# Attention begun with batch 0 alone; the other batches' residual, norm and turn, and the second feed-forward's norms, in pieces inside the slots

## The chip, the cores and the metric

One Trainium2 chip, one core. The metric is the device time of one execution in microseconds (us); the time before is the median of three runs. "Slot", "batch" and "half" are words of this kernel and are explained below.

## What is computed

A macaron block on x of 8 batches x 512 tokens x 128 features, all in fp32 accuracy:

```
x = x + 0.5 * ffn(layernorm(x))        # first feed-forward
x = x + attn(layernorm(x), Q, K, VO)   # 16 heads, softmax over 512 keys
x = x + 0.5 * ffn(layernorm(x))        # second feed-forward, same weights
ffn: 3 blocks of  h = h + lin2(gelu(layernorm(lin1(h))))
lin: dequantised 4-bit weight + low-rank part (folded into one 128 x 128 weight)
```

## The kernel before, in words

Every engine has its own program, written out by hand, and they meet on counting semaphores; there is no scheduler. x stays in SBUF as 32 tiles of 128 tokens, four tiles to a batch.

**Feed-forward.** `ffn(f)` is a software pipeline of 12 steps (3 blocks x 4 pairs of batches), one pair of batches a step. A step has `lin1`, `turn_z` and `lin2` on TensorE (PE), `squares` and `gelu` on ScalarE (ACT), `seed`, `z_scaled` and `step_h` on VectorE (DVE), and three Newton steps for 1/sqrt on GpSimd (POOL, `newton`: small linked operations on `u_t`, `u_u`, `u_rstd`). Ahead of it each batch is normalised (`norm_stats`, `norm_means`, `norm_sigmas`, `norm_apply`) and turned by four PE transposes (`pre`); behind it it is turned back (`post`) and added to x (`step_x`). Batches go in two groups of four.

**Between the first feed-forward and attention** batches 0 to 3 get `step_x`, their norm, `turn_xn` and their split in fp16 high and low halves (`halves_turned`, `split`, `halves_tokens`, `xn_low`); only then does attention start. Batches 4 to 7 are normalised in its first slots, and turned in slots 0 to 3.

**Attention** runs in slots, one head of one batch each, 128 in all, with six more ahead (-6 to -1) that fill the pipeline. PE's slot k has, in this order: `scores` of head k+1 (8 matmuls), `outputs` of head k-1 (12 small ones), `weigh` of head k (12, in pieces `weigh(0)` to `weigh(3)`), `maxima` for head k+4 or so (4) and one `project` (3): 39 matmuls. DVE's slot k has `row_max` of head k+2 (four stream transposes into `head_ops`), `scale_out`, two `reduce_max` (they follow `maxima` of the same slot), `y_low` of head k, and the low half of a projection. ACT's slot k has `exps` and `p_high` of head k+1, a projection's high half and `y_high` of head k. POOL's slot k has `add_out` of head k-3 (x plus the head's output) and `p_low` of head k, in two halves; `plo_done` counts them, and PE waits for the first ahead of `weigh(0)` of slot k. Since `exps` and `p_high` of head k are done in ACT's slot k-1, POOL's slot k lies about two thirds of a slot ahead of PE's slot k. Slots 4 to 119 are a hardware loop over four slots.

**Behind attention** the same DVE statements compute the norms of all 8 batches for `ffn(1)`: batches 0 to 3 in the last slots, 4 to 7 behind `lin1` of the first two steps.

Of the kernel before, what the change touches and what calls it, by code (L numbers as in the profile page):

```python
# [21 lines left out]
def macaron(nc, x_d, q_d, k_d, vo_d, qw_d, sc_d, bias_d, la_d, lb_d, gam_d, bet_d, out_d):  # L22
# [10 lines left out]
    GT = SG * TT  # L33
# [13 lines left out]
    with ctx:  # L47
# [42 lines left out]
        stats = sb("stats", [128, GT, 6])  # L90
        mv = sb("mv", [128, 2, GT, 2])
        var = sb("var", [128, GT])
        rs_t = sb("rs_t", [128, GT])
        rs_u = sb("rs_u", [128, GT])
        rstd = sb("rstd", [128, 2, GT])
        shift = sb("shift", [128, 2, GT])
# [35 lines left out]
        bank = [ps[:, b, :] for b in range(B)]  # L132
# [3 lines left out]
        pj_ps = ps[:, 5, :]  # L136
        o_ps = ps[:, 6:8, 0:2 * RW].rearrange("p b (t n) -> p b t n", n=RW)
# [24 lines left out]
        xhat_a = sem("xhat_a")  # L162
        pre_t = sem("pre_t")
# [42 lines left out]
        late_ps = ps[:, 6, :]  # L206
        top_rows = ps[0:NTOP, 0, 0:128]
        top_cols = ps[:, 2, 0:NTOP]

        def wait_xhat(eng, u, c):  # L210

            if c < SG // 2:
                eng.wait_ge(xhat_v, u * (SG // 2) + c + 1)
            else:
                eng.wait_ge(xhat_a, (u - 1) * (SG // 2) + c + 1)
# [25 lines left out]
        def _(sp):  # L241
# [60 lines left out]
            for b in range(B):  # L302
                sp.wait_ge(x1_ready, B + b + 1)
                sp.dma_start(ov[:, b * TT:(b + 1) * TT, :], x[:, b * TT:(b + 1) * TT, :]).then_inc(out_sem, 16)
# [4 lines left out]
        def _(pool):  # L309
# [39 lines left out]

            pool.wait_ge(prep_p, 8)  # L350
# [7 lines left out]
            pool.wait_ge(prep_a, 3)  # L358
            pool.tensor_tensor(w_lo[:, :, :], qk32[:, :, :], w_hi[:, :, :], ALU.subtract).then_inc(prep_p, 1)
            pool.wait_ge(prep_a, 5)  # L360
            pool.tensor_tensor(vo_lo[:, :, :], vo32[:, :, :], vo_hi[:, :, 0:D], ALU.subtract).then_inc(prep_p, 1)

            def xn_low(b):
                tiles = slice(b * TT, (b + 1) * TT)
                pool.wait_ge(xnh_ready, b + 1)
                pool.tensor_tensor(xn_lo[:, tiles, 0:D - 1], xhat[:, tiles, 0:D - 1], xn_hi[:, tiles, 0:D - 1],
                                   ALU.subtract).then_inc(xnl_ready, 1)

            for b in range(SG):
                xn_low(b)  # L370

            def p_low(k, par, a):
                pool.wait_ge(phi_done, 2 * k + (a + 1))
                rows = slice(2 * a, 2 * a + 2)
                pool.tensor_tensor(p_lo[:, par, rows, :], p32[:, par, rows, :], p_hi[:, par, rows, :],  # L376
                                   ALU.subtract).then_inc(plo_done, 1)

            def add_out(k, par, batch):
                pool.wait_ge(o_scaled, k + 1)  # L380
                rows = x[:, bass.ds(batch * TT, TT), :]
                pool.tensor_tensor(rows, rows, o_sb[:, par, :, :], ALU.add).then_inc(x_added, 1)  # L382

            def slot(k, j, add_batch):
                if not isinstance(k, int) or k >= 3:
                    if not isinstance(k, int) or k >= 4:
                        pool.wait_ge(x_added, k - 3)
                    add_out(k - 3, (j + 1) % 2, add_batch)
                for a in range(2):
                    if not isinstance(k, int) or k >= 2:  # L390
                        pool.wait_ge(av_half, 2 * (k - 2) + (a + 1))
                    p_low(k, j % 2, a)

            slot(0, 0, 0)
            slot(1, 1, 0)
            xn_low(SG)
            slot(2, 0, 0)
            xn_low(SG + 1)
            slot(3, 1, 0)  # L400
            xn_low(SG + 2)
            xn_low(SG + 3)
            with pool.Fori(1, NH // 4) as i:
                for j in range(4):
                    slot(4 * i + j, j, (4 * i + (j - 3)) // H)
            for k in range(NH - 3, NH):
                pool.wait_ge(x_added, k)
                add_out(k, k % 2, k // H)
            for i in range(STEPS):
                newton(1, i)  # L410

        @block.scalar
        def _(act):
# [7 lines left out]
            def pre(f, s):  # L421
                for c in range(SG):
                    b = s * SG + c
                    act.wait_ge(pre_t, f * B + b + 1)
                    nc.scalar.activation(hT[:, b, :], bank[b], ACT.Copy).then_inc(h0_ready, 1)

            def norm_apply(u, s, batches=range(SG // 2, SG)):

                act.wait_ge(moments_ready, u + 1)
                for c in batches:  # L430
                    for t in range(c * TT, (c + 1) * TT):
                        ins = nc.scalar.activation(xhat[:, s * GT + t, :], x[:, s * GT + t, :], ACT.Identity,
                                                   scale=rstd[:, s, t:t + 1], bias=shift[:, s, t:t + 1])
                    ins.then_inc(xhat_a, 1)

            def squares(f, i):
                for c, b in unit_batches(i):
                    act.wait_ge(lin1_done, at(f, i, c))
                    for t in range(TT):
                        cols = slice(t * D, (t + 1) * D)  # L440
                        ins = nc.scalar.activation(work_b[:, b, cols], bank[b][:, cols], ACT.Square,
# [3 lines left out]
            def gelu(f, i):  # L445
                n = i // UNITS
                for c, b in unit_batches(i):
                    act.wait_ge(z_turned, at(f, i, c))
                    nc.scalar.activation(work_a[:, b, :], bank[b], ACT.Gelu, scale=gam[:, n:n + 1],
                                         bias=bet[:, n:n + 1]).then_inc(gl_ready, 1)  # L450

            def weight_halves(i):

                if i == 7:
                    act.wait_ge(prep_v, 3)
                if i in (7, 8):
                    n = i - 7
                    ins = nc.scalar.activation(w_hi[:, n, :], qk32[:, n, :], ACT.Identity, scale=inv2[:, n:n + 1])
                if i == 9:
                    ins = nc.scalar.activation(vo_hi[:, :, 0:D], vo32[:, :, :], ACT.Identity, scale=inv2[:, 2:3])  # L460
                    ins.then_inc(prep_a, 1)
                if i == 10:
                    act.wait_ge(prep_a, 2)
                    for n in range(2):
                        ins = nc.scalar.activation(qk32[:, n, :], qk32[:, n, :], ACT.Identity, scale=inv2[:, n:n + 1])
                    ins.then_inc(prep_a, 1)
                if i == 11:
# [3 lines left out]
                    nc.scalar.activation(vo32[:, :, :], vo32[:, :, :], ACT.Identity,  # L471
                                         scale=inv2[:, 2:3]).then_inc(prep_a, 1)

            def halves_tokens(u, b):
                wait_xhat(act, u, b % SG)
                tiles = slice(b * TT, (b + 1) * TT)
                nc.scalar.activation(xn_hi[:, tiles, 0:D - 1], xhat[:, tiles, 0:D - 1], ACT.Copy).then_inc(xnh_ready, 1)

            def halves_turned(b, src):
                act.wait_ge(xn_t, b + 1)  # L480
                nc.scalar.activation(xt_hi[:, b, :], src, ACT.Copy).then_inc(xth_ready, 1)

            def ffn(f):
                if f == 0:
                    norm_apply(0, 0)
# [6 lines left out]
                for i in range(STEPS + 3):  # L492
                    if i >= 3:
                        gelu(f, i - 3)
# [663 lines left out]
```

## Time and profile before

| | |
|---|---|
| median of 3 runs | 1027.19 us (1026.61 to 1031.52) |
| the profiled execution: its own time / its span | 1026.52 us / 1024.7 us |
| PE busy | 963.4 us, 94% |
| DVE busy | 877.1 us, 86% |
| ACT busy | 802.6 us, 78% |
| POOL busy | 784.4 us, 77% |
| PE's share of the chain that ended last | 83% (DVE 10%, ACT 3%, POOL 2%) |
| granted TensorE clock, mean | 0.979 |

The span is the profiled program from its first to its last instruction; the execution's own time is 1.8 us longer. [...] Times in rows are counted from the span's start.

### The profile page before, as it was taken

The page shows a single profiled execution, that of the slowest core. Times are in us where ns is not written, and L with a number is a line of the kernel's source. Part 1 is how long each engine was busy: PE and PEld are TensorE (multiplying, and loading weights), DVE is VectorE, ACT ScalarE, POOL GpSimd, SP SyncE. Part 2 cuts the span into 40 slices and gives each one's busy share as a digit, 9 for nine tenths or more (in the row PEclk, how much of TensorE's full clock was granted, in tenths as well). Part 3 has the DMA queues.
Part 4 walks back from the last instruction along what each step waited for, and adds up shares of the span by engine and source line. Part 5 has one row for each costly group of instructions (what it writes and reads, how often), then busy time and mean ns, then how long its engine had stood idle before and what let it go on. Part 6 is the DMA issues. An engine that isn't in the chain of part 4 may idle for free.

```text
span 1024.7 us, 22051 instructions
## 1 busy us (share of the span) xinstructions
PE 963.4 (94%) x5892; PEld 502.3 (49%) x5892; DVE 877.1 (86%) x1786; ACT 802.6 (78%) x1293; POOL 784.4 (77%) x706
## 2 busy tenths in 40 slices
PE   4895689999999999999999999999999999997897
PEld 4763234444444444444444444444444444444775
DVE  7667898988888889898888888888888888898566
ACT  4885388888888888888888888888888888886874
POOL 2644168888888888888888888888888888886442
PEclk9999699999999999999999999999999999998999
DMA  9000222222222222222222222222222222220002
GB/s 244 1 2 0 51 50 55 62 61 62 63 63 64 64 65 63 64 64 63 63 64 65 63 64 61 61 61 61 61 61 61 61 61 61 61 62 1 1 1 83
DMA packets 71676, 59.03 MB, mean 58 GB/s; under 512 B 11168, under 2 KB 70560, under 8 KB 71648
## 3 DMA queue, kind: packets, MB, share of 16 engines
q1 hardware_dynamic: 71392, 58.31, 24.0%
q10 hardware_dynamic: 256, 0.39, 0.1%
q8 instruction: 12, 0.20, 0.1%
q14 instruction: 16, 0.13, 0.0%
HBM read 6.23 MB, written 2.10 MB: 8 GB/s over the span
## 4 chain that ended last, share of the span: by engine, by line
PE 83%; DVE 10%; ACT 3%; POOL 2%; issue 1%; DMA 1%; SPq 0%; DVEq 0%; POOLq 0%; ACTq 0%
PE ps L1032 11%; PE ps L1034 10%; PE ps L1033 10%; PE ps L1022 10%; PE ps L1023 10%; PE ps L1015 6%; PE ps L1007 3%; PE ps L953 3%; PE ps L1048 3%; PE ps L1044 3%; PE ps L1045 3%; PE ps L1009 3%; PE ps L1008 3%; PE ps L925 2%; DVE stats L654 1%
## 5 line engine op out<-in xcount | busy, mean ns | idle before, releaser
L376 POOL TENSOR_TENSOR p_lo<-work_b,p_hi 128x1024 f16<-128x1024 f32 x256 | 539.8, 2130 | 129.4 <-ACT p_hi L527 129.3
L794 DVE TENSOR_REDUCE mcol<-ps 128x2 f16<-128x1024 f32 x256 | 301.0, 1220 | 0.8 <-PE ps L1015 0.7
L522 ACT ACTIVATE work_b<-ps,exp_scale 128x1024 f32<-128x1024 f32 x256 | 271.6, 1111 | 32.4 <-PE ps L1023 32.3
L527 ACT ACTIVATE p_hi<-work_b 128x1024 f16<-128x1024 f32 x256 | 256.0, 1054 | 0.0
L1022 PE MATMUL ps<-head_ops 128*128 128x512 f16 x512 | 195.1, 381 | 4.1 <-DVE mcol L794 2.0
L1032 PE MATMUL ps<-p_hi,xn_hi 128*128 128x512 f16 x512 | 195.2, 381 | 0.0
L1023 PE MATMUL ps<-head_ops 128*128 128x512 f16 x512 | 195.1, 381 | 0.0
L1033 PE MATMUL ps<-p_hi,xn_lo 128*128 128x512 f16 x512 | 194.4, 380 | 0.0
L1034 PE MATMUL ps<-p_lo,xn_hi 128*128 128x512 f16 x512 | 194.3, 379 | 0.0
L382 POOL TENSOR_TENSOR x<-x,o_sb 128x512 f32 (+1 forms) x128 | 162.7, 1271 | 8.7 <-DVE o_sb L819 8.7
L804 DVE STREAM_TRANSPOSE head_ops<-mcol 32x128 f16<-32x128 f16 x512 | 155.5, 304 | 9.3
L532 ACT ACTIVATE y_hi<-ps 128x512 f16<-128x512 f32 x128 | 76.5, 598 | 90.0 <-PE ps L1034 89.8
L810 DVE TENSOR_TENSOR y_lo<-ps,y_hi 128x512 f16<-128x512 f32 x128 | 88.5, 691 | 60.5 <-ACT y_hi L532 60.4
L1044 PE MATMUL ps<-vo_hi,y_hi 128*128 (+1 forms) x512 | 93.8, 221 | 5.6 <-DVE o_sb L819 5.6
L819 DVE TENSOR_TENSOR o_sb<-ps,rinv 128x512 f32<-128x512 f32 x128 | 88.4, 691 | 7.0
L1048 PE MATMUL ps<-vo_hi,y_lo 128*128 (+1 forms) x512 | 93.9, 221 | 0.3 <-DVE y_lo L810 0.2
L1045 PE MATMUL ps<-vo_lo,y_hi 128*128 (+1 forms) x512 | 93.8, 220 | 0.0
L1015 PE MATMUL ps<-pair_ops 64*128 64x512 f16 x512 | 79.8, 386 | 8.0 <-DVE mcol L794 4.9
L1022 PEld LDWEIGHTS ps<-head_ops 128*128 128x128 f16 x512 | 50.2, 98 | 68.8 <-issue 6.5
L1034 PEld LDWEIGHTS ps<-p_lo,xn_hi 128*128 (+1 forms) x512 | 50.2, 98 | 60.8 <-issue 0.6
L1023 PEld LDWEIGHTS ps<-head_ops 128*128 128x128 f16 x512 | 50.2, 98 | 59.6 <-issue 0.8
L1032 PEld LDWEIGHTS ps<-p_hi,xn_hi 128*128 (+1 forms) x512 | 50.1, 98 | 59.5 <-issue 22.1
(116 smaller groups left out, 1316.9 us busy)
## 6 DMA issues: line engine op xcount, KB each, us to landing
head_ops<-pair_ops SPq DMA_DIRECT2D x512, 64.0 KB, 2.0
head_ops<-pair_ops SPq DMA_DIRECT2D x128, 128.0 KB, 2.4
x<-x_dram SPq DMA_DIRECT2D x8, 256.0 KB, 5.9
out<-x SPq DMA_DIRECT2D x8, 256.0 KB, 3.0
vo_last<-wvo_dram SPq DMA_DIRECT2D x1, 1024.0 KB, 13.5
qk<-wq_dram SPq DMA_DIRECT2D x1, 512.0 KB, 5.6
qk<-wk_dram SPq DMA_DIRECT2D x1, 512.0 KB, 6.4
scl<-scales_dram ACTq DMA_DIRECT2D x8, 48.0 KB, 5.2
```

Of the source, the lines that this page charges most:

```text
L376: pool.tensor_tensor(p_lo[:, par, rows, :], p32[:, par, rows, :], p_hi[:, par, rows, :], ALU.subtract).then_inc(plo_done, 1)
L382: pool.tensor_tensor(rows, rows, o_sb[:, par, :, :], ALU.add).then_inc(x_added, 1)
L522: nc.scalar.activation(p32[:, par, 2 * a:2 * a + 2, :], s_ps[a], ACT.Exp, scale=exp_scale[:, 0:1]).then_inc(exp_done, 1)
L527: nc.scalar.activation(p_hi[:, par, 2 * a:2 * a + 2, :], p32[:, par, 2 * a:2 * a + 2, :], ACT.Copy).then_inc(phi_done, 1)
L794: nc.vector.tensor_reduce(mcol[:, par, :, t, 0], s_ps[t % 2], AX.X, ALU.max, negate=True).then_inc(max_red, 1)
L804: ins = nc.vector.transpose(rows[:, :, 32 * q:32 * q + 32], mcol[32 * q:32 * q + 32, par, e, :, :])
L1015: ins = nc.tensor.matmul(s_ps[t % 2][:, e, :], pair_ops[half, buf, 0, t * 128:(t + 1) * 128], pair_ops[half, buf, 2, :], start=True, stop= ...
L1022: nc.tensor.matmul(s_ps[a][:, u % 2, :], k1[:, ring, keys], q1[:, ring, :], start=True, stop=False)
L1023: ins = nc.tensor.matmul(s_ps[a][:, u % 2, :], k2[:, ring, keys], q2[:, ring, :], start=False, stop=True)
L1032: nc.tensor.matmul(y_ps, xh, p_hi[:, par, u, :], start=(u == 0), stop=False)
L1033: nc.tensor.matmul(y_ps, xl, p_hi[:, par, u, :], start=False, stop=False)
L1034: ins = nc.tensor.matmul(y_ps, xh, p_lo[:, par, u, :], start=False, stop=(u == TT - 1))
```

## The change

The functions `attn_slot(n)` and `ffn_slot(m)` give for every batch the slot at which its pieces begin, and each engine's new `late(k)` does the pieces that fall on slot k, at one place inside its slot. Batch 0 alone is finished between the first feed-forward and attention. The last two steps of the first feed-forward overlap slots -6 to -4. The first two `lin1` steps of the second feed-forward run inside slot 127. All slots are written out (no loop), on all engines but the DMA queue. In the slots the norm's 1/sqrt is split: DVE does the variance and the first guess (`late_seed`), POOL three Newton steps in five parts, one part a slot (`late_newton`), ACT applies it. The last group's norm and the eight `step_x` of the second feed-forward are reordered. ACT's scaling of the attention weights goes to DVE.

```diff
+        def attn_slot(n):
+            return 16 * (n - 1) - 8 if n > 1 else -3
+        def ffn_slot(m):
+            return 16 * (m + 1) + 5
+        SEEDS = sorted([(attn_slot(n) + 4, "attn", n) for n in range(1, B)] +
+                       [(ffn_slot(m) + 2, "ffn", m) for m in range(B - 1)])
...
 # POOL
+            def late_newton(kind, b, part):
+                tiles = slice(b * TT, (b + 1) * TT)
+                y, v = rstd[:, tiles], var[:, tiles]
+                if part == 0:
+                    if seeded(kind, b) > 1:
+                        pool.wait_ge(nrstd_ready, seeded(kind, b) - 1)
+                    pool.wait_ge(nseed_ready, seeded(kind, b))
+                for n in range(3 * part, min(3 * part + 3, 12)):
+                    if n % 4 == 0:
+                        plink(pool, pool.tensor_tensor(n_t[:, :], y, y, ALU.mult))
...
+            def late(k):
+                for part in range(5):
+                    for n in late_at(k, 4 + part, "attn"):
+                        late_newton("attn", n, part)
+                    for m in late_at(k, 2 + part, "ffn"):
+                        late_newton("ffn", m, part)
+                for h in range(2):
+                    for n in late_at(k, 11 + h, "attn"):
+                        xn_low(n, h)
+            def slot(k):
+                if k >= 3:
+                    add_out(k - 3)
+                if k >= 0:
+                    for a in range(2):
+                        if k >= 2:
+                            pool.wait_ge(av_half, 2 * (k - 2) + (a + 1))
+                        p_low(k, a)
+                late(k)
-            for b in range(SG):
-                xn_low(b)
...
 # DVE
+            def late_seed(b):
+                tiles = batch_tiles(b)
+                norm_means(tiles)
+                link(dve, nc.vector.tensor_scalar(var[:, tiles], mv[:, tiles, 1], LN_EPS, None, ALU.add))
+                nc.vector.tensor_scalar(rstd[:, tiles].bitcast(I32), var[:, tiles].bitcast(I32), -0.5, MAGIC,
+                                        ALU.mult, ALU.add).then_inc(nseed_ready, 1)
...
+            def late(k):
+                for h in range(2):
+                    for n in late_at(k, h, "attn"):
+                        step_x_half(n, h, late_ps)
+                    for n in late_at(k, 2 + h, "attn"):
+                        dve.wait_ge(x1_ready, 2 * n + h + 1)
+                        norm_stats(half_tiles(n, h))
+                    for n in late_at(k, 11 + h, "attn"):
+                        split(n, h, late_ps)
+                    for m in late_at(k, h, "ffn"):
+                        dve.wait_ge(x_added, HPB * (m + 1))
+                        norm_stats(half_tiles(m, h))
+                for n in late_at(k, 4, "attn"):
+                    late_seed(n)
+                for m in late_at(k, 2, "ffn"):
+                    late_seed(m)
...
 # ACT
+            def late(k):
+                for h in range(2):
+                    for n in late_at(k, 9 + h, "attn"):
+                        act.wait_ge(nrstd_ready, seeded("attn", n))
+                        apply_half(n, h, xat_a)
+                    for n in late_at(k, 10 + h, "attn"):
+                        halves_tokens(n, h)
+                    for n in late_at(k, 11 + h, "attn"):
+                        halves_turned(n, h, late_ps)
+                    for m in late_at(k, 7 + h, "ffn"):
+                        act.wait_ge(nrstd_ready, seeded("ffn", m))
+                        apply_half(m, h, xff_a)
+                    for m in late_at(k, 9 + h, "ffn"):
+                        pre_half(m, h, late_ps)
...
 # PE
+            def late_turn(k, src, h, done, sem_read, count):
+                pe.wait_ge(*late_reader[0])
+                if k >= 1:
+                    pe.wait_ge(o_scaled, k)
+                turn_half(late_ps, src, h, done)
+                late_reader[0] = (sem_read, count)
+            def late(k):
+                for h in range(2):
+                    for n in late_at(k, h, "attn"):
+                        late_turn(k, h_tile(n), h, post_t, x1_ready, 2 * n + h + 1)
+                    for n in late_at(k, 11 + h, "attn"):
+                        wait_attn_xhat(pe, n, h)
+                        late_turn(k, x_tile(n), h, xn_t, xsplit_done, 2 * n + h + 1)
+                    for m in late_at(k, 9 + h, "ffn"):
+                        pe.wait_ge(xff_a, 2 * m + h + 1)
+                        late_turn(k, x_tile(m), h, pre_t, h0_ready, B + 2 * m + h + 1)
```

**POOL, around slot 12.** Before, in the loop (x is the sum of `add_out`, `p_lo` the two `p_low`; the ISA and REGISTER_ALU rows carry waits):

```order
L382 ISA [waits o_scaled,x_added]
L382 TENSOR_TENSOR x<-x,o_sb 128x512
L374 ISA [waits av_half]
L376 TENSOR_TENSOR p_lo<-work_b,p_hi 128x1024 [waits phi_done]
L374 REGISTER_ALU [waits av_half]
L376 TENSOR_TENSOR p_lo<-work_b,p_hi 128x1024 [waits phi_done]
L382 ISA [waits o_scaled,x_added]
L382 TENSOR_TENSOR x<-x,o_sb 128x512
```

Of the change, slots 12 and 13 (`n_t` and `n_u` are the Newton steps' tiles):

```order
L463 TENSOR_TENSOR x<-x,o_sb 128x512 [waits o_scaled,x_added]
L454 TENSOR_TENSOR p_lo<-work_b,p_hi 128x1024 [waits phi_done,av_half] x2
L425 TENSOR_TENSOR n_t<-rstd 128x4 [waits nseed_ready,nrstd_ready]
L427 TENSOR_TENSOR n_u<-n_t,var 128x4 [waits pch]
L429 TENSOR_SCALAR n_t<-n_u 128x4 [waits pch]
L463 TENSOR_TENSOR x<-x,o_sb 128x512 [waits o_scaled,x_added,pch]
L454 TENSOR_TENSOR p_lo<-work_b,p_hi 128x1024 [waits phi_done,av_half] x2
```

The first Newton part stands between the two `p_low` of slot 12 and `add_out` and `p_low` of slot 13, and it waits for DVE's seed.

**DVE, slot 12 of the change.** Where that seed is made (`mcol` are the two `reduce_max`, `rstd` the seed):

```order
L910 STREAM_TRANSPOSE head_ops<-mcol 32x4x32 x3
L923 RECIPROCAL rinv<-ps 128x4 [waits o_done,o_scaled]
L927 TENSOR_TENSOR o_sb<-ps,rinv 128x512 [waits x_added,vch]
L899 TENSOR_REDUCE mcol<-ps 128x2 [waits max_mm] x2
L743 BN_AGGR mv<-stats 128x2 x4
L773 TENSOR_SCALAR var<-mv 128x4 [waits vch]
L774 TENSOR_SCALAR rstd<-var 128x4 [waits vch]
L916 TENSOR_TENSOR y_lo<-ps,y_hi 128x512 [waits yh_ready]
```

The BN_AGGR and the two TENSOR_SCALAR rows are new; the others stand in this order in the loop of before too. The seed comes behind both `reduce_max` of slot 12.

## Rows read from the trace of the kernel before

**Rows 1.** Windows: busy us (x instructions) per engine, clock, DMA share, GB/s.

```profile
171.65:296.90 125.25, 125.25 (x779) 59.75 (x778) 111.94 (x200) 104.08 (x120) 108.39 (x61) 1.00 0.27 63
```

**Rows 2.** Timeline, PE, two slots: start, us, engine line op, operands.

```profile
504.84 0.38 PE L1022 MATMUL ps<-head_ops 128*128 128x512 f16 x1
...
511.13 0.38 PE L1022 MATMUL ps<-head_ops 128*128 128x512 f16 x1
...
513.54 0.38 PE L1032 MATMUL ps<-p_hi,xn_hi 128*128 128x512 f16 x1
```

**Rows 3.** Timeline, PE, from the first feed-forward to slot 5.

```profile
84.77 1.98 PE L953 MATMUL ps<-work_a,wt 128*128 128x512 f32 x4 [2.56 <-ACT work_a L449]
...
101.89 3.85 PE L895 MATMUL ps<-ident,work_a 128*128 128x128 f32 x16 [7.51 <-DVE work_a L671]
...
134.28 0.38 PE L1022 MATMUL ps<-head_ops 128*128 128x512 f16 x1 [0.86 <-DVE mcol L794]
...
171.65 0.38 PE L1022 MATMUL ps<-head_ops 128*128 128x512 f16 x1
```

**Rows 4.** Timeline, PE, behind attention.

```profile
929.88 0.39 PE L1022 MATMUL ps<-head_ops 128*128 128x512 f16 x1 [0.87 <-DVE head_ops L804]
...
940.61 0.27 PE L1044 MATMUL ps<-vo_hi,y_hi 128*128 128x129 f16 x1 [5.56 <-DVE o_sb L819]
...
956.54 0.66 PE L895 MATMUL ps<-ident,work_a 128*128 128x128 f32 x4 [3.70 <-DVE work_a L671]
...
960.14 0.63 PE L922 MATMUL ps<-bias_rows,ones_b 128*128 128x512 bf16 x1
```

**Rows 5.** Timeline, DVE: `z_scaled` of step 10, then the norm of batches 0 to 3.

```profile
82.32 1.28 DVE L715 TENSOR_TENSOR work_b<-ps,u_rstd 128x512 f32<-128x512 f32 x2
...
97.14 1.17 DVE L659 BATCH_NORM_AGGREGATE mv<-stats 128x2 f32<-128x6 f32 x16
...
100.64 0.17 DVE L664 SCALAR_TENSOR_TENSOR shift<-mv,rstd 128x16 f32<-128x16 f32 x1
```

**Rows 6.** Groups by line: count, busy us, mean ns, idle before.

```profile
L722 DVE SCALAR_TENSOR_TENSOR hT<-ps,bias,hT 128x512 f32<-128x512 f32 x48 | 35.6, 749 | 28.2 <-PE ps L953 26.0
```

**Rows 7.** Timeline, DVE, one slot.

```profile
507.05 1.26 DVE L804 STREAM_TRANSPOSE head_ops<-mcol 32x128 f16<-32x128 f16 x4
...
509.17 2.35 DVE L794 TENSOR_REDUCE mcol<-ps 128x2 f16<-128x1024 f32 x2
512.02 0.69 DVE L810 TENSOR_TENSOR y_lo<-ps,y_hi 128x512 f16<-128x512 f32 x1 [0.50 <-ACT y_hi L532]
```

**Rows 8.** Timeline, DVE, and then POOL, last slots.

```profile
932.68 1.19 DVE L605 TENSOR_SCALAR rstd<-var 128x16 int32<-128x16 int32 x1
...
934.32 1.99 DVE L610 SCALAR_TENSOR_TENSOR rstd<-rs_u,rstd 128x16 f32<-128x16 f32 x1
...
934.16 4.20 POOL L376 TENSOR_TENSOR p_lo<-work_b,p_hi 128x1024 f16<-128x1024 f32 x2 [0.32 <-ACT p_hi L527]
```

**Rows 9.** The chain that ended last: start, us, engine, tile, line, count.

```profile
945.83 1.75 PE ps L895 x16
...
969.37 0.89 PE ps L925 x8
...
1014.66 2.48 DVE x L731 x4
```

**Rows 10.** Timeline, POOL, one slot.

```profile
502.76 4.21 POOL L376 TENSOR_TENSOR p_lo<-work_b,p_hi 128x1024 f16<-128x1024 f32 x2 [0.84 <-ACT p_hi L527]
506.94 1.26 POOL L382 TENSOR_TENSOR x<-x,o_sb 128x512 f32 x1
```

**Rows 11.** Timeline, POOL: small linked operations of a Newton step.

```profile
77.75 0.20 POOL L338 TENSOR_TENSOR u_t<-u_rstd 128x8 f32<-128x8 f32 x1 [1.49 <-DVE u_rstd L707]
...
78.60 0.20 POOL L341 TENSOR_TENSOR u_rstd<-u_rstd,u_t 128x8 f32<-128x8 f32 x1
```

**Rows 12.** Timeline, ACT, one slot.

```profile
511.39 0.60 ACT L532 ACTIVATE y_hi<-ps 128x512 f16<-128x512 f32 x1 [0.76 <-PE ps L1034]
```

More of the change, by code:

```diff
@@ L377, in p_low, with add_out @@
                                    ALU.subtract).then_inc(plo_done, 1)
-            def add_out(k, par, batch):
+            def add_out(k):
+                if k >= 1:
+                    pool.wait_ge(x_added, k)
                 pool.wait_ge(o_scaled, k + 1)
[L381 to L392, printed above, removed]
@@ L395, in _ @@
[L395 to L409, printed above, removed]
+                b = k // HPB
@@ new lines, in slot @@
+            def slot(k):
[7 more added lines that the diff above has]
+                late(k)
+            for k in range(-6, NH):
+                slot(k)
+            add_out(NH - 3)
+            newton(1, 0)
+            add_out(NH - 2)
+            add_out(NH - 1)
@@ L410, in _ @@
+            for i in range(1, STEPS):
                 newton(1, i)
@@ L584, in _ @@
[L584 to L594 removed]
+            for k in range(-6, NH - 1):
+                slot(k)
+                if k == -5:
+                    gelu(0, STEPS - 1)
+                if k == -4:
+                    halves_tokens(0, 0)
+                    halves_tokens(0, 1)
@@ L681, in _ @@
+            norm_input(0)
             dve.wait_ge(w_in, 16 * 6)
@@ new lines, in _ @@
+            for h in range(2):
+                step_x_half(0, h, half_of(bank[0][0], h))
+            dve.wait_ge(x1_ready, 2)
+            norm_stats(batch_tiles(0))
+            norm_means(batch_tiles(0))
+            norm_sigmas(batch_tiles(0))
+            dve.wait_ge(moments_ready, 3)
+            norm_apply(half_tiles(0, 0))
+            z_scaled(0, STEPS - 1)
+            for h in range(2):
+                split(0, h, half_of(bank[0][1], h))
+            step_h(0, STEPS - 3, 0)
+            step_h(0, STEPS - 3, 1)
@@ L1116, in _ @@
-            pe.wait_ge(xnl_ready, B)
-            pe.wait_ge(xsplit_done, B)
-            with pe.Fori(1, NH // 4 - 2) as i:
-                for j in range(4):
-                    slot(i, 4 * i + j, j, 4 + j, NH - 12 + j)
-            for k in range(NH - 8, NH + 1):
-                slot(k // 4, k, k % 4, k, k)
-                if k == NH - 1:
-                    pre(1, 0)
-            ffn(1)
+                        maxima(pair % 2, 2 * (k % 2) + a)
+                if k % 2 == 0 and 0 <= k < NH:
+                    weigh(k, 1)
@@ new lines, in slot @@
+                if k + 6 - k % 2 < NH:
+                    project_pair(k)
+                late(k)
+                if 0 <= k < NH:
+                    pe.wait_ge(plo_done, 2 * k + 2)
+                    weigh(k, 2)
+                    weigh(k, 3)
+            pe.wait_ge(prep_a, 3)
+            pe.wait_ge(prep_p, 10)
+            for k in SLOTS:
+                if k == NH - 1:
+                    pe.wait_ge(exp_done, 2 * NH)
+                slot(k)
+                if k == -5:
+                    turn_z(0, STEPS - 1)
+                if k == -4:
+                    lin2(0, STEPS - 1)
@@ L1129 @@
+            post(B - 2)
+            post(B - 1)
 def kernel(**inputs):
```

862 lines of the change are left out of this document (461 added, 401 removed).

## The prediction

> **What bounds the kernel now.** I read the windows first. From 171.65 us to the last slots PE is busy all the time at full clock: 779 matmuls, 39 a slot, in 125.25 us, and DVE, POOL and ACT are busy 89, 87 and 83% of it [rows 1]. The timeline of PE gives the slot, 504.84 to 511.13, 6.29 us, and its array never rests in it [rows 2]. So in about 121 of 128 slots nothing can be won but only lost: PE work put into a slot costs its full length, and any wait that the other engines' buffers do not cover is lost for good. What can be won lies at the two ends. Ahead of attention PE waits 2.56 and 7.51 us, slot 0 starts at 134.28, and slot 5 at 171.65, so slots 0 to 4 take 37.4 instead of 31.4 us [rows 3]. Behind it PE waits 5.56 and 3.70 us [rows 4]. Both times DVE's norms stand in the way.
>
> **Start: 23.5 us won.** DVE sets the pace from the end of `z_scaled` of step 10 (82.32 + 1.28 = 83.6 [rows 5]) to slot 0. In the changed order it has to do: batch 0's residual (0.7), four statistics (0.85), aggregates (0.4), the 1/sqrt chain (from 98.31, where the aggregates end, to 100.81, 2.5 us, in the same rows), its half of the apply (0.5); `z_scaled` 1.3; split, with a wait, 0.9; six `step_h` at 0.75 [rows 6], 4.5; four pairs' worth of `reduce_max` less the last one's half, three and a half times 2.35, and two `row_max` of 1.26 [rows 7]; five projection lows at 0.6 and two half residuals at 0.4, 3.8, and small waits, 0.5. Slot 0 then starts at 114.0, slot 5 at 114.0 + 31.4 + 1.3 (the first seed's wait, below; there is no `add_out` behind it yet) + 1.4 (some slow clock behind a start with so little PE work) = 148.1, that is 23.5 us earlier than 171.65. Bounds: 27 without the contention, 19 if the low-activity start keeps the clock down twice as long.
> [...]
>
> **End: about 17 us won.** Slot 126 starts at 929.88 [rows 4], `lin1` of step 4 of the second feed-forward at 969.2 [rows 9], 39.4 us later; from there on it is PE-bound. In the new order I count from slot 126: weighing 5.0, `outputs(126)` to 7.2, four batches of `lin1` at 1.1 to 11.7, weighing of slot 127 to 14.5, `y_high`, `y_low` and `outputs(127)` to 16.0, `lin1` of step 2 to 18.2, `turn_z(0)`, a table load and `gelu(0)`, `lin2(0)` to 23.3, the last batch's norm on DVE until 24.6, `turn_z(1)` and the turn to 25.5, `lin1` of step 3 to 27.7. That is 11.7 us less; 1.0 more comes from the statistics that leave slot 125. At the very end the first four `step_x` (2.48 us) no longer stand ahead of the last `step_h` [rows 9]; with the shorter last pair 4.3 us. Bounds 12 and 20.
>
> **PE work moved into slots: 8.8 us lost.** Sixteen transposes take 1.75 us [rows 9], 0.22 for a half batch of two. Six batches' two turns (24 halves), batch 1's second turn (2) and seven batches' turn for the second feed-forward (14) are 40 halves in slots that are full: 8.8.
>
> **The seeds: 41 us lost.** This is the term that decides. POOL's slot k ends well before DVE's slot k comes to its seed. Take the slot of PE that begins at 504.84 as slot k: its `p_low` ran from 502.76 to 506.94 [rows 10]. DVE ends its second `reduce_max` of slot k at 511.50 [rows 7]. Aggregates and two linked operations take 0.8 (0.37 for four of the sixteen aggregates of 1.17 with their fixed part, 0.2 for each further one with its link [rows 5]): the seed is there at 512.30, and POOL has stood since 506.94 in front of it. Behind it are queued, in this order, the part's three small operations (77.75 to 78.60 for three, 0.85 [rows 11]), `add_out` (1.26) and the first `p_low` of slot k+1 (2.1) [rows 10], and PE waits for that one ahead of `weigh(0)`, which is due at 513.54 [rows 2]. POOL sees it 0.14 us later, as elsewhere. The `p_low` comes at 512.44 + 0.85 + 1.26 + 2.12 + 0.06 = 516.73. PE is late by 3.2 us; the cover was the 2.4 us from the end of a slot's first `p_low` (502.76 + 2.11 = 504.87) to `weigh(0)` of that slot (513.54 - 6.29 = 507.25), and the wait is 5.5. There are 14 seeds, one in slot 1 (counted above), six for attention and seven for the second feed-forward: 13 x 3.2 = 41.2 us. POOL gains nothing back in the slots behind: its idle time is 0.84 us a slot [rows 10], a part takes 0.85. The odd slots are taken like the even ones. Bounds: 1.6 each if half the wait is somehow met by PE being late already, 3.5 if the small operations are slower in a busy slot.
>
> **The clock: 11 us lost.** After the wait of 7.51 us the sixteen transposes took 3.85 us instead of 1.75 [rows 3, 9]: granted clock 0.50. After 3.70 us a bias matmul took 0.63 instead of 0.38 [rows 4], after 2.56 us nothing slowed (four `lin2` in 1.98) [rows 3]. The new waits, 3.2, lie between. A drop cost some 3.4 us at half speed, 1.7; I take half of that for each of 13, 11 us, with nothing and 22 as bounds.
>
> **Small terms: 7 us lost.** In slots 8 and 9 two late turns meet; the second waits for the first's reader on DVE, behind `reduce_max`, 1.9 us each: 3.8. ACT has 0.76 us ahead of `y_high` [rows 12]; slots with an apply and a split (1.17) are over it by 0.2 to 0.4, seven times. POOL without slack passes jitter on, 1 or 2 us: together 3. DVE's half residuals and statistics (0.4 to 0.5) fit its 0.50 [rows 7] and cost nothing; with the cover gone they would cost their length.
>
> **The sum** against the profiled execution's own time, 1026.5 us: - 23.5 - 17 + 8.8 + 41.2 + 11 + 6.8 = + 27.3, that is **1054 us**. The median of the runs is 0.7 above that execution, which is within the error.
>
> **Rivals.**
> (a) *The seeds' wait is met.* If POOL's slot lay later against DVE's than I read, or PE were late by as much from other work, the 41 and the 11 us fall away: 1026.5 - 40.5 + 8.8 + 6.8 = 1002, faster by 2.4%. Against it: `p_low` of slot k must be done before PE weighs head k, `reduce_max` of slot k cannot begin before PE's `maxima`, which comes later, and the order of instructions has nothing between. It decides from a wait of 2.4 us down. Chance 0.15.
> (b) *Half waits.* 1.6 us each and no clock drop: 1026.5 - 40.5 + 8.8 + 20.6 + 6.8 = 1022. Chance 0.08.
> (c) *Every seed drops the clock*: 1065. Chance 0.15.
> (d) *DVE waits instead of POOL*: the seed's operations stand behind a `p_low` as in [rows 8] and `y_low` comes 1.2 us late: 13 x 1.2 = 16 in place of 41 and 11, 1018. For it the 1.99 us; against it that POOL is idle at that moment. Chance 0.04.
> My forecast has 0.58.
> [...]
>
> **Range and chances.** The likeliest case alone spans 1040 to 1065 (start 19 to 27, end 12 to 20, clock 0 to 22). With (c) and the edge of (b) the range is 1022 to 1068. A difference of 0.5%, 5 us, is about what a measurement of this kernel can tell from none. Faster holds (a), most of (d) and part of (b): 0.18; within 0.5% the rest of (b): 0.06; slower 0.76.
>
> **What would show it.** In the changed profile POOL's idle time should have 13 waits of about 5.5 us for DVE's seed, PE 13 waits of about 3 us at the first `weigh` matmul for `p_low`, in slots 12, 23, 28, 39 and so on plus one, and slots of 9.5 us there. Slot 0 should start near 114. If PE's waits for `p_low` are absent, (a) is right; if granted clock in the middle stays 1.00, the clock term is nothing. The forecast is wrong if the start wins much more than 27 us or the unrolled code itself costs time in ordinary slots.

## The result, and the profile after

The changed kernel takes 1064.16 us (median of 4 runs, 1060.76 to 1067.6), the kernel before 1026.97 beside it (median of 4). The ratio is 1.0352, with a 95% interval of 1.0301 to 1.0402: slower. The profiled execution took 1060.76 us, its span is 1058.8.

The waits of POOL and of PE in the changed kernel: engine and line, what was waited for, us in total, times, the longest. The kernel before had neither of the first two.

```profile
POOL n_t L425 <- DVE rstd L774: 74.2, 14, 5.3
PE ps L1155 <- POOL p_lo L454: 40.2, 14, 3.0
```

One seed, in the timelines of DVE, POOL and PE: start, us, engine, line, operands, and in brackets the idle time before and what ended it.

```profile
204.14 2.35 DVE L899 TENSOR_REDUCE mcol<-ps 128x2 f16<-128x1024 f32 x2
206.40 0.37 DVE L743 BATCH_NORM_AGGREGATE mv<-stats 128x2 f32<-128x6 f32 x4
206.81 0.17 DVE L773 TENSOR_SCALAR var<-mv 128x4 f32<-128x4 f32 x1
207.01 0.17 DVE L774 TENSOR_SCALAR rstd<-var 128x4 int32<-128x4 int32 x1
```
```profile
207.32 0.20 POOL L425 TENSOR_TENSOR n_t<-rstd 128x4 f32<-128x4 f32 x1 [5.31 <-DVE rstd L774]
...
208.17 1.27 POOL L463 TENSOR_TENSOR x<-x,o_sb 128x512 f32<-128x512 f32 x1
209.39 4.22 POOL L454 TENSOR_TENSOR p_lo<-work_b,p_hi 128x1024 f16<-128x1024 f32 x2
```
```profile
211.58 0.39 PE L1155 MATMUL ps<-p_hi,xn_hi 128*128 128x512 f16 x1 [2.98 <-POOL p_lo L454]
```

DVE's seed is there at 207.18, POOL has stood for 5.31 us in front of it (before, it went straight on to `add_out` at this place [rows 10]), then come the piece, `add_out` and the first `p_low`, and PE starts its first weighing 2.98 us late. The seed slot takes 9.44 us instead of 6.29.

The start, in PE's timeline, which answers [rows 3], and the same time on DVE:

```profile
93.73 1.09 PE L1024 MATMUL ps<-ident,work_a 128*128 128x128 f32 x4 [7.39 <-DVE work_a L754]
...
117.49 0.38 PE L1147 MATMUL ps<-head_ops 128*128 128x512 f16 x1
```
```profile
88.88 2.06 DVE L700 SCALAR_TENSOR_TENSOR rstd<-rs_u,rstd 128x4 f32<-128x4 f32 x1
90.97 1.97 DVE L748 SCALAR_TENSOR_TENSOR shift<-mv,rstd 128x4 f32<-128x4 f32 x1
```
```profile
88.87 4.05 POOL L406 TENSOR_TENSOR vo_lo<-vo,vo_hi 128x1024 f16<-128x1024 f32 x2
```

The last two fences show the contention: two small DVE operations, 2.06 and 1.97 us long (the same lines take 0.16 each in e3, where no `vo_low` stands beside them), end at 90.94 and 92.94, POOL's two `vo_low` of 2.0 us each by 92.92.

The end, in PE's timeline, which answers [rows 4]: slot 126 starts in the first row, `lin1` of step 4 in the last.

```profile
974.58 0.38 PE L1147 MATMUL ps<-head_ops 128*128 128x512 f16 x1
...
997.36 1.99 PE L1085 MATMUL ps<-work_a,wt 128*128 128x512 f32 x4 [2.45 <-ACT work_a L541]
...
1003.26 0.38 PE L1054 MATMUL ps<-bias_rows,ones_b 128*128 128x512 bf16 x1
```

The clock behind another seed, in windows of 1 us: window, its length, PE busy and matmuls, granted clock, DMA share, GB/s. PE rests from 281.4 to 284.4; the clock (granted, as a share of full speed) falls when it already works again, and stays at the lower level, 0.50, for 3.4 us; a matmul of `weigh` takes 0.63 us there instead of 0.38.

```profile
282.87:283.87 1.00, 0.00 (x0) 1.00 0.65 130
283.87:284.87 1.00, 0.47 (x3) 1.00 0.63 135
284.87:285.87 1.00, 1.00 (x7) 0.82 0.39 84
285.87:286.87 1.00, 1.00 (x5) 0.50 0.66 135
...
288.87:289.87 1.00, 1.00 (x6) 0.97 0.00 0
```

By slots the time went as follows (start of slot 5 and of slot 122 by PE's timeline, before and after):

| stretch | before | after | difference | predicted |
|---|---|---|---|---|
| start of the span to slot 5 | 171.65 | 150.76 | -20.9 | -23.5 |
| slot 5 to slot 122 | 735.54 | 801.96 | +66.4 | +67.8 |
| slot 122 to the end | 117.5 | 106.1 | -11.4 | -17 |

Of the 66.4 us in the middle, 38.6 are PE's waits for `p_lo` (40.2 less 1.6 of the first seed, which lies ahead of slot 5). The clock is 12.5: 8 of the 13 seed slots take 10.9 to 11.3 instead of 9.44 us, 1.4 to 1.6 each beyond their turns. The half turns are 8.4: 38 of the 40 lie in this stretch (the other two in slots 126 and 127), and a slot with one takes 6.51 instead of 6.29. The double turns are 4.1 (slots 8 and 9 took 8.92 and 8.64), and 2.8 are the rest.

### The profile page after: what moved, and what is told of

It reads as the page before. It is cut to its first block, busy times and chain, and to the rows that moved or that the text cites. A ratio compares the mean times of both kernels' runs of the same rounds, so it can differ in the third digit from the quotient of the medians.

```text
span 1058.8 us, 19251 instructions
## 1 busy us (share of the span) xinstructions
PE 971.8 (92%) x5892; PEld 501.6 (47%) x5892; DVE 872.7 (82%) x1782; ACT 809.1 (76%) x1343; POOL 824.9 (78%) x912
## 4 chain that ended last, share of the span: by engine, by line
PE 74%; DVE 13%; POOL 6%; issue 4%; ACT 1%; DMA 1%; DVEq 0%; SPq 0%; POOLq 0%; ACTq 0%
PE ps L1155 10%; PE ps L1157 10%; PE ps L1156 9%; PE ps L1147 8%; PE ps L1148 8%; PE ps L1140 6%; DVE mcol L899 4%; PE ps L1085 3%; PE ps L1132 3%; POOL p_lo L454 3%; PE ps L1057 3%; PE ps L1133 2%; PE ps L1134 2%; PE ps L1174 2%; PE ps L1170 2%
## 5 line engine op out<-in xcount | busy, mean ns | idle before, releaser
L1155 PE MATMUL ps<-p_hi,xn_hi 128*128 128x512 f16 x512 | 197.1, 385 | 40.6 <-POOL p_lo L454 40.2
L1156 PE MATMUL ps<-p_hi,xn_lo 128*128 128x512 f16 x512 | 196.6, 384 | 0.0
L1157 PE MATMUL ps<-p_lo,xn_hi 128*128 128x512 f16 x512 | 196.5, 384 | 0.0
L463 POOL TENSOR_TENSOR x<-x,o_sb 128x512 f32<-128x512 f32 x128 | 162.9, 1273 | 6.5 <-DVE o_sb L927 2.1
L1155 PEld LDWEIGHTS ps<-p_hi,xn_hi 128*128 128x128 f16 x512 | 50.3, 98 | 99.0 <-POOL p_lo L454 42.9
L1170 PE MATMUL ps<-vo_hi,y_hi 128*128 128x129 f16 x512 | 93.8, 220 | 1.5 <-ACT y_hi L614 1.5
L1174 PE MATMUL ps<-vo_hi,y_lo 128*128 128x129 f16 x512 | 93.5, 221 | 0.9 <-DVE y_lo L916 0.8
L1171 PE MATMUL ps<-vo_lo,y_hi 128*128 128x128 f16 x512 | 93.8, 219 | 0.0
L1157 PEld LDWEIGHTS ps<-p_lo,xn_hi 128*128 128x128 f16 x512 | 50.6, 99 | 61.9 <-issue 2.6
```

The source lines that it names most:

```text
L463: pool.tensor_tensor(rows, rows, o_sb[:, k % 2, :, :], ALU.add).then_inc(x_added, 1)
L1155: nc.tensor.matmul(y_ps, xn_hi[:, row, :], p_hi[:, k % 2, u, :], start=(u == 0), stop=False)
L1156: nc.tensor.matmul(y_ps, xn_lo[:, row, :], p_hi[:, k % 2, u, :], start=False, stop=False)
L1157: ins = nc.tensor.matmul(y_ps, xn_hi[:, row, :], p_lo[:, k % 2, u, :], start=False, stop=(u == TT - 1))
```

## The experiments

Beside the experiments, which ran on four chips, the kernel before had medians of 1029.7 to 1030.8 us, not 1026.97. So what is compared are the ratios to the kernel before on the same chip; "on the first scale" is the ratio times 1027. Theory: POOL waits in order for a seed that DVE makes late in its slot, this wait goes on to PE, and PE's rest drops the clock. Rivals: the pieces' own length on a POOL without slack; and (d) of the prediction, DVE blocked by `p_low`.

**e1: POOL a slot later.**

```diff
-                    for n in late_at(k, 4 + part, "attn"):
+                    for n in late_at(k, 5 + part, "attn"):
-                    for m in late_at(k, 2 + part, "ffn"):
+                    for m in late_at(k, 3 + part, "ffn"):
```

> POOL takes each piece of the Newton steps one slot later (offset 5 + part instead of 4 + part, 3 + part instead of 2 + part), so that it comes to the seed some 6.3 us later, 0.9 us behind DVE. Theory (a wait of POOL for a seed that DVE makes late): PE's 14 waits for p_lo (40.2 us in the profile of the changed kernel) and the 8 clock drops behind them (13 us; 16 in the median) go, nothing else moves: 1064.2 - 40 - 16 = about 1008, seed slots 6.3 to 6.5 us. Rival (d) of the prediction: POOL is now inside a p_low when DVE makes the seed, DVE's small operations wait for its end, y_low comes 1.2 us late 13 times: about 1024. Rival (pieces cost by themselves, wherever they stand): POOL has no slack for them and each of the 5 pieces still delays the next p_low: above 1035.

Measured: 1026.57 us (8 runs), ratio 0.9963 (0.9947 to 0.9979), 1023 on the first scale. All waits for `p_lo` and all clock drops between slot 5 and the last slots are gone (granted clock 1.00). The view of PE's waits has a new first row:

```profile
PE ps L1174 <- DVE y_lo L916: 16.8, 16, 1.1
```

The timelines of DVE and POOL in a seed slot of e1:

```profile
206.85 0.37 DVE L743 BATCH_NORM_AGGREGATE mv<-stats 128x2 f32<-128x6 f32 x4
207.25 1.52 DVE L773 TENSOR_SCALAR var<-mv 128x4 f32<-128x4 f32 x1
208.81 0.17 DVE L774 TENSOR_SCALAR rstd<-var 128x4 int32<-128x4 int32 x1
208.89 0.68 DVE L916 TENSOR_TENSOR y_lo<-ps,y_hi 128x512 f16<-128x512 f32 x1
```
```profile
204.53 4.22 POOL L454 TENSOR_TENSOR p_lo<-work_b,p_hi 128x1024 f16<-128x1024 f32 x2 [0.83 <-ACT p_hi L609]
```

L773 takes 1.52 instead of 0.17 us: it ends at 208.77, POOL's `p_low` at 208.75. `y_low` comes 1.4 us late and PE waits 1.14. So the theory accounts for the first wait but not for the time, which it alone put at 1008: rival (d), to which the prediction gave 0.04, is what appears once that wait is gone, and 1024 was expected for it. The pieces' own length is not what costs (above 1035 was expected for that).

**e2: a smaller dose.** The piece stands behind the next slot's `add_out`:

```diff
                     add_out(k - 3)
+                late_parts(k)
                 if k >= 0:
...
-                    for n in late_at(k, 4 + part, "attn"):
+                    for n in late_at(k, 5 + part, "attn"):
                         late_newton("attn", n, part)
-                    for m in late_at(k, 2 + part, "ffn"):
+                    for m in late_at(k, 3 + part, "ffn"):
                         late_newton("ffn", m, part)
```

`late_parts` is the loop over the five parts, taken out of `late`, which keeps `xn_low` and stays where it is.

> A smaller dose of the same wait: the pieces stand in POOL's queue behind the next slot's add_out and ahead of its first p_low, 1.26 us further back. Theory: the wait at the seed falls from 5.3 to about 4.0 us, PE's wait for the p_low from 3.0 to about 1.75 in each of 13 slots (- 16 us). If the clock drops follow from the length of PE's wait, all go as well, as after 2.56 us ahead of attention: 1064.2 - 16 - 16 = about 1031. If they come from something else in these slots, 8 to 12 stay: about 1048.

Measured: 1035.96 us (5 runs), ratio 1.0048 (1.0028 to 1.0067), 1032 on the first scale. In the view of PE's waits:

```profile
PE ps L1158 <- POOL p_lo L454: 25.2, 16, 1.8
```

The seed slots take 8.2 us (8.4 with a turn in them), and none of the 13 shows a clock drop. The theory's 1031 holds, the 1048 of unmoved drops doesn't.

**e3: the start's contention.** As e1, with POOL's `xn_low(0, 0)` and `xn_low(0, 1)` ahead of the two `vo_low`.

> As e1, and POOL's two vo_low stand behind batch 0's two xn_low, so that no long POOL operation lies on DVE's 1/sqrt chain of batch 0. Theory (contention of 3.7 us at the start): the two operations that took 2.06 and 1.97 us take 0.16, and slot 0 starts 3.7 us earlier: 3.7 us below e1. Rival: the start hangs on something else by then (ACT's apply, PE at half clock), and less than 1.5 us is won.

Measured: 1022.16 us (4 runs), ratio 0.9921 (0.9902 to 0.9940), against 1026.57 for e1: 4.4 us less, and in the trace slot 0 starts at 115.07 instead of 118.42, 3.4 us earlier. Where a start lies differs by a microsecond or so from one execution to the next (117.49, 118.42 and 118.88 in the changed kernel, e1 and e2, whose programs are the same up to there). Counted from the end of DVE's `z_scaled` of step 10, slot 0 comes 33.0 us later in e1 and 28.8 in e3. So the contention at the start had about the 3.7 us that the prediction gave it.

**e4: the turns apart.**

```diff
-            return 16 * (n - 1) - 8 if n > 1 else -3
+            return 16 * (n - 1) - 6 if n > 1 else -3
```

> As e3, and the pieces of batches 2 to 7 begin two slots later, so that batch 2's two turns don't meet batch 1's second turn in slots 8 and 9. Theory: slots 8 and 9 (8.92 and 8.63 us in the changed kernel) fall to about 6.5 each, 4 to 4.6 us below e3. Rival: the long slots come from something else (the first seed, ACT's apply), and nothing is won; or the moved pieces meet ACT's long slots and lose 1 or 2 us.

Measured: 1017.10 us (4 runs), ratio 0.9873 (0.9855 to 0.9891), 5.1 us below e3. Slots 8 and 9 take 6.59 and 6.51 us instead of 8.91 and 8.64 in e3, which is 4.5 of it.

**e5: a place without either wait.** As e4, with each piece between the next slot's two `p_low`:

```diff
                         p_low(k, a)
+                        if a == 0:
+                            late_parts(k)
```

> As e4, but each Newton piece stands in the next slot between POOL's first and second p_low. Theory (two waits, one place each): POOL stands in front of the seed while DVE makes it, so no p_low lies on DVE's two small operations (1.52 and 0.17 us in e1 become 0.17 and 0.17) and PE's waits of 1.1 us for y_lo go (15.5 us in e4); the piece delays the second p_low to 4 us behind the slot's start, PE wants it only at its third weighing, 5.5 us behind it, so PE waits for no p_lo either. Seed slots 6.3 to 6.5 us, 15 us below e4: about 1002, ratio 0.973. Rival: the lateness of POOL, which has no slack in these slots, comes out at the next slot's first p_low (cover 2.4 us, late by 1.0 by my reading) and PE waits there: between e4 and e1.

Measured: 1001.24 us (4 runs), ratio 0.9726 (0.9705 to 0.9746); 0.973 was expected. In a seed slot, in the timelines of DVE and of POOL, DVE's two operations take 0.17 us again, and POOL's wait is short and between two `p_low`. The third fence is all that PE waits for `p_lo` in the whole run:

```profile
209.98 0.17 DVE L777 TENSOR_SCALAR var<-mv 128x4 f32<-128x4 f32 x1
210.18 0.17 DVE L778 TENSOR_SCALAR rstd<-var 128x4 int32<-128x4 int32 x1
```
```profile
207.25 2.13 POOL L454 TENSOR_TENSOR p_lo<-work_b,p_hi 128x1024 f16<-128x1024 f32 x1 [0.84 <-ACT p_hi L613]
210.49 0.20 POOL L425 TENSOR_TENSOR n_t<-rstd 128x4 f32<-128x4 f32 x1 [1.11 <-DVE rstd L778]
...
211.34 2.13 POOL L454 TENSOR_TENSOR p_lo<-work_b,p_hi 128x1024 f16<-128x1024 f32 x1
```
```profile
PE ps L1159 <- POOL p_lo L454: 1.2, 3, 0.7
```

No slot from 1 on is longer than 6.59 us, and slots 5 to 121 take 745.4 us, 9.8 more than before: the 38 half turns (8.4) and 1.4 us. Together with e7, which doesn't differ from it, this is the fastest version, 2.7% below the kernel before and some 6% below the changed one.

**e6: the other engine moves.** As e4, with DVE's seed behind `y_low`.

```diff
                 late(k)
...
                     y_low(k)
+                late_seeds(k)
```

`late_seeds` is the loop over `late_seed`, taken out of `late`.

> As e4, but DVE makes the seed behind y_low instead of ahead of it; it is still blocked by the p_low that runs then, for some 0.8 us. Theory (the 1.1 us are y_low's place behind the blocked operation): y_lo comes in time, PE's waits for it go, some 12 to 15 us below e4. Rival: DVE has 0.5 us of slack in a slot and 1.4 us of extra work, so that lateness goes on to row_max and reduce_max of the next slot, and PE waits there about as long: within 5 us of e4.

Measured: 1006.78 us (4 runs), ratio 0.9756 (0.9731 to 0.9781), 12 us below e4 by the ratios. DVE's timeline in a seed slot:

```profile
213.03 0.69 DVE L916 TENSOR_TENSOR y_lo<-ps,y_hi 128x512 f16<-128x512 f32 x1 [0.44 <-ACT y_hi L614]
213.64 0.37 DVE L743 BATCH_NORM_AGGREGATE mv<-stats 128x2 f32<-128x6 f32 x4
214.04 0.39 DVE L773 TENSOR_SCALAR var<-mv 128x4 f32<-128x4 f32 x1
```

The operation is still blocked, 0.39 us instead of 0.17, until `p_low` ends at 214.40, but nothing that PE waits for stands behind it. The block cost time mainly by its place ahead of `y_low`; hardly any of the lateness is handed on (PE's waits for `mcol` at the scores sum to 2.2 us in 6 waits). The middle, slots 5 to 121, still takes 750.5 us, 5.1 more than in e5.

**e7: the tail.** As e5, with the last turns and `step_x` as in the kernel before: those of batches 0 to 3 together ahead of the last `lin2` and `step_h`, the others behind.

> As e5, but the last turns and step_x stand as in the kernel before: four batches' turns and step_x ahead of the last lin2 and step_h, four behind them. My prediction gave the changed order of the tail 4.3 us; the trace of the changed kernel shows 0.1 (from lin1 of step 4 to the end 55.6 us, before 55.5). If that reading holds, e7 is within 1 us of e5; if the order is worth 4.3 us and something else took them away, e7 is 4 us slower.

Measured: 1002.14 us (4 runs), ratio 0.9718 (0.9700 to 0.9736), against 0.9726 for e5: no difference. The order of the tail is worth nothing that these runs can tell, and not 4.3 us.

**e8: a larger dose.** The changed kernel with `late_seeds(k)` as the last thing in DVE's slot.

> As the changed kernel, but DVE makes the seed last in its slot, behind y_low and the pair's low half, 1.3 us later. Theory (POOL's wait goes on to PE in full, and the clock drops with the length of PE's wait): PE's wait for p_lo grows from 3.0 to about 4.3 us in 14 slots (+ 18 us), and the clock drops behind all 13 instead of 8 to 12 (1.65 us each, + 2 to 8): about 1087, ratio 1.058. If the clock's drops have nothing to do with the wait's length, their number stays 8 to 12 and the time about 1082.

Measured: 1103.89 us (4 runs), ratio 1.0710 (1.0692 to 1.0727), above what either expected. By the view of waits they grew by 1.7 instead of 1.3 us:

```profile
POOL n_t L425 <- DVE rstd L774: 98.5, 14, 7.0
PE ps L1158 <- POOL p_lo L454: 64.4, 14, 4.7
```

and the clock falls in all 13 seed slots, while PE still rests. The seed slots take 12.6 to 14.0 us; the 9.44 of the changed kernel with a wait of 4.69 instead of 2.97, and a turn of 0.22 in some, account for 11.2 to 11.4, so the clock costs 1.4 to 2.8 us each time. Windows of 1 us behind one of them:

```profile
217.31:218.31 1.00, 0.00 (x0) 1.00 0.02 5
218.31:219.31 1.00, 0.00 (x0) 0.61 0.00 0
...
224.31:225.31 1.00, 1.00 (x3) 0.50 0.00 0
225.31:226.31 1.00, 1.00 (x6) 0.97 0.00 0
```

Direction and mechanism are as the theory has them, the size is not: the wait grew by more, and its price for a drop (1.65 us) holds only for 6 of the 13. In the other 7 the lower level lasts 6.8 instead of 3.4 us, and they cost 2.2 to 2.8 us each.

**e9: wait or work.** The changed kernel without the twelve operations of the Newton steps (the seed's rough value is used in their place):

```diff
-                for n in range(3 * part, min(3 * part + 3, 12)):
+                for n in range(0):
```

> As the changed kernel, but the twelve small operations of the Newton steps are left out (the seed's rough value is used); POOL's wait for the seed, the last piece's shift and everything else stay. It asks which share of PE's wait is the wait itself and which the 0.85 us of the pieces: PE's waits for p_lo fall from 3.0 to about 2.15 us (- 12 us). Waits of 1.75 us left the clock alone (e2), of 3.0 dropped it behind 8 of 13 seeds, of 4.6 behind all (e8): without drops 1064.2 - 12 - 16 = 1036, with all as before 1052. Rival (the pieces, not the wait, make PE late): the waits all but go, below 1025.

Measured: 1043.94 us (4 runs), ratio 1.0135 (1.0112 to 1.0158), 1041 on the first scale. PE's waits are as worked out:

```profile
PE ps L1155 <- POOL p_lo L454: 28.4, 14, 2.1
```

4 of the 13 seed slots have a drop (10.2 to 10.4 us, the others 8.6 to 8.8), so the time lies between the 1036 expected without drops and the 1052 with all. Of PE's 3.0 us the piece is 0.85 and the wait for the seed the rest.

**e10: the clock alone, first try.** The changed kernel with 16 transposes, which nobody reads, behind `outputs` in the 13 slots behind a seed:

```diff
+                if k - 1 in [key[0] for key in SEEDS] and k > 2:
+                    pe.wait_ge(*late_reader[0])
+                    pe.wait_ge(o_scaled, k)
+                    for t in range(16):
+                        nc.tensor.transpose(late_ps[:, t % 2, :], ident[:, :], ident[:, :])
```

> As the changed kernel, but in the 13 slots behind the seeds (all but the first) PE does 16 more transposes of the identity into an unread piece of PSUM, behind its outputs and ahead of the first weighing, that is inside its wait for p_lo: 1.75 us of work that nobody reads. Theory (the clock drops because PE's array rests for these 3.0 us, the wait itself comes from POOL): the seed slots keep their 9.4 us, but the 11 us ones (8 of 13) fall to 9.4 too, granted clock 1.00 from slot 5 to the last: 13 to 16 us below the changed kernel, about 1050, ratio 1.022. If the drops come from elsewhere, 8 to 12 slots of 11 us stay and the time is 1064; if the added work delays PE, the time is above it.

Measured: 1078.86 us (4 runs), ratio 1.0470 (1.0444 to 1.0495). That is the last of the outcomes named, a time above 1064: the added work delays PE, because it waits for DVE first, as PE's timeline shows:

```profile
213.37 3.54 PE L1240 MATMUL ps<-ident 128*128 128x128 f32 x16 [2.14 <-DVE o_sb L927]
```

After a rest of 2.14 us the transposes take 3.54 us instead of 1.75, at a mean granted clock of 0.53. 9 of the 13 slots are about 12.0 to 12.3 us long, the other 4 about 10.4 to 10.6. The rest was moved, not filled.

**e11: the clock alone.** The same transposes go into `y_ps`, which the next weighing overwrites. Their one wait is for DVE's `y_low` of the slot before, which is there by then. Against e10:

```diff
-                    pe.wait_ge(*late_reader[0])
-                    pe.wait_ge(o_scaled, k)
+                    pe.wait_ge(yl_ready, k)
...
+                        cols = slice(128 * (t % 2), 128 * (t % 2) + 128)
-                        nc.tensor.transpose(late_ps[:, t % 2, :], ident[:, :], ident[:, :])
+                        nc.tensor.transpose(y_ps[:, cols], ident[:, :], ident[:, :])
```

> e10's added transposes waited 2.1 us for DVE, so PE rested just as long ahead of them and the clock fell in 9 of 13 slots. Here the same 16 transposes go into y_ps, which the next weighing overwrites, right behind outputs and with no wait of their own: PE works 1.75 us more and rests 3.0 - 1.75 = 1.25 us. Theory (the clock falls behind a rest of PE, oftener the longer it is: 0 of 13 at 1.75 us, 4 at 2.1, 8 at 3.0, 13 at 4.6): no drop, all 13 seed slots 9.4 us, granted clock 1.00 from slot 5 to the last, 1047 to 1051, ratio 1.019 to 1.022. If drops come from elsewhere (the time between seeds, the DMA beside it), 4 to 9 slots of 11 us stay and the time is 1055 to 1065.

Measured: 1051.22 us (4 runs), ratio 1.0204 (1.0173 to 1.0235), below 1.0352 although PE does 208 transposes more. POOL still waits for the seeds (68.4 us in 14 waits, at most 5.3), PE's own waits in the seed slots fall to 1.24 us, the seed slots take 9.44 to 9.46 us (9.67 with a turn), and the clock holds, here in one window over the middle:

```profile
153.00:950.00 797.00, 777.28 (x4899) 385.19 (x4896) 694.23 (x1340) 643.74 (x802) 686.18 (x551) 1.00 0.28 60
```

So the drops come from PE's rest and from nothing else in these slots. By the ratios they are worth about 15 us of the changed kernel's 37 (12.5 in its trace, with 8 drops).

## Why the prediction came out

Forecast 1054, measured 1064.16, inside the range of 1022 to 1068; slower had 0.76. The profiled execution, 1060.76, is 6.8 us above the forecast: 2.6 from the start and 5.6 from the end, less 1.4 in the middle. In the middle two small misses partly cancel: the seeds' waits cost 2.6 us less than forecast, the clock 1.5 more.

- **What bounds it, and the seeds' wait (41.2).** Right in mechanism and size: 14 waits of POOL of 5.3 us (5.5 was read), 13 of PE of 3.0 (3.2), in the slots named, together 38.6 us. e1, e2, e8 and e9 move the wait to 0, 1.75, 4.7 and 2.1 us, and the time moves with it.
- **The clock (11).** The step that took half of 13 drops was near for the profiled execution (8 drops, 12.5 us), but the number of drops was a guess between none and all, not a reading. Runs of the same kernel fall into 1060.8 and 1061.6 us with a mean granted clock of 0.978, and 1066.7 and 1067.6 with 0.972. Four more drops would cost 4 x 1.65 = 6.6 us, which fits, and the median would then contain about 10 drops, 16 us. This is not shown: there is a trace of the first kind only, and the kernel before, which has no seeds in its slots, spreads about as far (1026.3 to 1032.7 us beside e11, mean clock 0.979 to 0.974), so the difference could lie at the ends as well.
- **The start (-23.5).** Measured -20.9, between the bounds 19 and 27. The contention was right (2.06 and 1.97 us, and e3). Slot 0 began at 117.5, not 114.0. Of that, 1.2 us are there before the chain starts (`z_scaled` of step 10 ended at 84.84, not at 83.6). 2.0 are the term "small waits, 0.5", which was sized too small: DVE waits 0.76 us for ACT's `xt_hi` and 1.77 for its `pair_ops`, because PE ran at the lower clock there (0.50 from 91 to 97 us; four `lin2` in 3.46 us instead of 1.88). In e4, where the granted clock is 1.00 in this stretch, the same two waits are 0.30 each. Slots 0 to 4 then took 33.3 us instead of the 34.1 counted.
- **The end (-17).** Measured -11.4, just outside the bounds of 12 and 20. Slot 126 to `lin1` of step 4 took 28.7 us, 10.7 less than the 39.4 of before (11.7 was worked out), and slots 122 to 125 took 0.8 less (1.0). The failed step is "at the very end ... 4.3 us": from `lin1` of step 4 on both kernels take the same time, 55.5 us before and 55.6 after. e7 shows that the order makes no difference. The reason I give is a reading of the traces, not an experiment: I had followed DVE's chain, but PE is busy for 49 to 50 of these 55.5 us in either order, with the same 32 transposes, and what DVE no longer does between was done beside PE's work.
- **PE work in slots (8.8)** and **double turns (3.8)**: right. Slots with a half turn take 6.51 us, 0.22 more; e5's middle is 9.8 us longer than before; e4 gives 4.5 us back for slots 8 and 9.
- **Rivals.** (a), no wait, 1002: not this kernel, but its sum is that of e5, 0.9726 times 1027 = 999 (e5 has in addition the 3.7 and 3.8 us of e3 and e4 mended, and its two ends gain less than was forecast, so that the two numbers meet partly by chance). (b), half waits, is out: the waits were 3.0 us, not 1.6. (c), all drops, 1065, is nearer to the median than the forecast is, but by luck: the trace shows 8 drops of 13, and what fills the gap is the 8.2 us that the ends gained less. (d) was argued away because POOL is idle when the seed is made; that is right for this kernel and is why the 1.1 us don't appear in it. Each of the two waits hides the other: whoever takes away POOL's wait puts a `p_low` on DVE's operation. In the trace of e1 that operation takes 1.52 us and ends 0.02 us behind the `p_low`; the operations of 1.19 and 1.99 us in [rows 8] end within 0.04 us of `add_out` and of a `p_low` too. The four aggregates ahead of it ran inside the same `p_low` in 0.37 us, as long as in the changed kernel, where POOL stands still at this place. What it is that holds the one and not the others, no run shows.

The gain that the change was built for is there, about 32 us at both ends, and was lost by where one piece stands in POOL's queue: its 14 waits (40.2 us) and the drops behind them (12.5 in the trace) cost 53 us, the work moved 8.8.

## What to carry to other kernels

Before a dependent piece of work is put into the slots of a pipeline, place its producer and its consumer on one time axis. An in-order engine that runs ahead of its producer by most of a slot passes the wait, less its cover, to everything behind (the changed kernel: of POOL's 5.3 us PE got 3.0); the same piece further back in its queue, where the producer is all but done, costs next to nothing (e5: 1.4 us besides the turns).

When one wait is taken away, ask what the engine does in the time that it gains: here, in e1, it computes, and the producer's small operation is held until that computing ends (1.52 instead of 0.17 us). Look for a place where the engine stands still for the short time in which the other works, or move what is blocked behind the operation that matters (e6).

Price a new rest of PE with the clock behind it (here a drop cost 1.4 to 1.6 us behind a rest of 3.0, 1.4 to 2.8 behind 4.7). Judge a new order of work in the tail of a kernel by the engine that is busy there: the order that shortened DVE's chain gave nothing here (e7).

## What the runs showed of the hardware

The clock's answer to a rest is not the same each time. Seed slots with a drop, by PE's rest: 0 of 13 at 1.1 us (e1), at 1.2 (e11) and at 1.75 (e2), 4 of 13 at 2.12 (e9), 9 of 13 at 2.14 (e10), 8 of 13 at 3.0 (the changed kernel), 13 of 13 at 4.7 (e8). Ahead of attention 2.56 us left it alone once [rows 3]. At 3.0 us the granted clock fell about 1 us after PE had begun to work again (284.4 and 285.5 in the windows above), so the same wait can look harmless in its own window. Runs of the changed kernel, with some seeds that drop the clock and some that don't, spread from 1060.8 to 1067.6 us; those of e11, where none does in the trace, from 1050.9 to 1052.1. That the seeds make this spread is not shown (the kernel before spreads by 6 us without them).

DVE's one-input operation from SBUF to SBUF on 128x4 elements took 1.52 us instead of 0.17 beside POOL's `p_low` and ended with it (e1), while four aggregates (0.37 us), `reduce_max` out of PSUM (2.35 us for two) and `y_low` (0.69, in e6) ran beside `p_low` at their usual lengths.
